# A fused cross-attention, attention and expert block: two rounds of open rows in line, the first layer norm's scaling on GpSimd

## What is computed

```
x = x + xattn(layernorm(x), ctx)     # channel gate
x = x + attn(layernorm(x))           # 32 heads of 64, 8 kv heads, causal, 64 tokens
x = x + ffn(layernorm(x))            # dense 2048 x 2048 + top-2 of 8 low-rank experts
```

```
_, topk_idx = jax.lax.top_k(cm, k)                  # cm: (16, 2048, 1601), k = 38
mask = zeros(B, L, C).at[b_idx, l_idx, topk_idx].set(1.0)
crucial = mask * x ; rest = (1 - mask) * x
# max and mean of both over the 64 channels -> conv of 7 taps -> norm -> sigmoid -> gate
```

## Time and profile before

| | us |
|---|---|
| median of 3 runs | 2354.77 (2352.66 to 2357.07) |
| the profiled execution, time | 2347.9 |
| the profiled execution, span | 2346.1 |
| PE busy / DVE busy / ACT busy / POOL busy in the span | 1996.5 / 1431.2 / 1008.6 / 930.0 |

### The profile page before, as it was taken

How to read it: one execution, slowest core, us unless ns; L and a number is a source line. 1 busy time by engine, 2 the same in 40 slices (tenths; PEclk the granted TensorE clock), 3 DMA queues, 4 the chain that set the end, 5 groups by cost and what they waited for, 6 DMA issues and landing times. The chain is left out here.

```text
span 2346.1 us, 39096 instructions
## 1 busy us (share of the span) xinstructions
PE 1996.5 (85%) x15210; PEld 1633.0 (70%) x15210; DVE 1431.2 (61%) x2343; ACT 1008.6 (43%) x2006; POOL 930.0 (40%) x855
## 2 busy tenths in 40 slices
PE   4777788788882054899999999999999999999999
PEld 4666566667762044688787888887778888878887
DVE  6999899999998898764444550134445524731111
ACT  6777767677771036432322332222333422522221
POOL 1221111112220150466554555555555535644554
PEclk9999899899996577999999999999999999999999
DMA  9999787789980203452225444322235436434443
GB/s 366 373 363 325 271 281 264 249 313 326 321 300 15 85 1 99 157 153 80 75 82 172 138 140 125 99 82 81 77 128 162 152 103 209 138 112 130 141 143 120
DMA packets 150088, 407.69 MB, mean 174 GB/s; under 512 B 15376, under 2 KB 36112, under 8 KB 148112
## 3 DMA queue, kind: packets, MB, share of 16 engines
q1 hardware_dynamic: 149616, 403.55, 50.7%
q0 software_dynamic: 288, 1.64, 0.2%
HBM read 379.96 MB, written 25.17 MB: 173 GB/s over the span
## 5 line engine op out<-in xcount | busy, mean ns | idle before, releaser
L1158 POOL TENSOR_TENSOR t<-t,t 128x512 fp32r<-128x512 f32 (+1 forms) x488 | 651.1, 1345 | 676.7 <-ACT t L1151 676.3
L1704 PE MATMUL ps<-t,t 128*128 128x512 f32 x1856 | 739.7, 399 | 19.7 <-POOL t L1158 9.4
L1706 PE MATMUL ps<-t,t 128*128 128x512 f32 x1856 | 725.4, 391 | 0.0
L1705 PE MATMUL ps<-t,t 128*128 128x512 f32 x1856 | 724.9, 391 | 0.0
L1151 ACT ACTIVATE t<-t 128x512 fp32r<-128x512 f32 (+1 forms) x488 | 295.5, 608 | 704.5 <-PE ps L1706 384.1
L704 PE MATMUL ps<-t,t 128*128 128x128 bf16 (+1 forms) x6656 | 454.0, 224 | 165.7 <-DVE t L442 155.1
L704 PEld LDWEIGHTS ps<-t,t 128*128 128x128 bf16 x6656 | 403.3, 101 | 266.7 <-DVE t L442 216.5
L442 DVE TENSOR_SCALAR t<-t,t 128x1601 bf16<-128x1601 f32 x512 | 515.7, 1050 | 3.6 <-DVE t L615 0.4
L665 ACT ACTIVATE t<-t,t 128x1601 bf16<-128x1601 f32 x256 | 416.5, 1627 | 79.4 <-DVE t L598 77.3
L1704 PEld LDWEIGHTS ps<-t,t 128*128 128x128 f32 x1856 | 349.3, 188 | 100.5 <-POOL t L1158 14.0
L1706 PEld LDWEIGHTS ps<-t,t 128*128 128x128 f32 x1856 | 349.2, 188 | 74.1
(11 more groups left out here) (214 smaller groups left out, 1698.9 us busy)
## 6 DMA issues: line engine op xcount, KB each, us to landing
t<-ctxT SPq DMA_DIRECT2D x256, 800.5 KB, 5.9
t<-wqkv SPq DMA_DIRECT2D x192, 256.0 KB, 3.2
t<-wo SPq DMA_DIRECT2D x128, 256.0 KB, 4.6
t<-wb SPq DMA_DIRECT2D x128, 256.0 KB, 3.3
t<-xT SPq DMA_DIRECT2D x32, 256.0 KB, 6.6
t<-xT SPq DMA_DIRECT2D x2, 4096.0 KB, 12.1
t<-x1d SPq DMA_DIRECT2D x32, 256.0 KB, 4.9
x2d<-t SPq DMA_DIRECT2D x32, 256.0 KB, 2.0
```

Source lines behind the costliest of these rows:

```text
L1158: e.tensor_tensor(wlo[r][:, 0:nk, :], raw[r][:, 0:nk, :], wh[r][:, 0:nk, :].bitcast(F32), ALU.subtract).then_inc(w_lo, 1)
L1704: e.matmul(bank[:, :], wh[r][:, q, :], xl, start=(kt == 0), stop=False)
L1705: e.matmul(bank[:, :], wlo[r][:, q, :], xh, start=False, stop=False)
L1706: m = e.matmul(bank[:, :], wh[r][:, q, :], xh, start=False, stop=(c == NCH[p] - 1 and q == nk - 1))
```

## The change

Two rounds of the open rows stand in line ahead of the loop, with buffers of their own (ring buffers 5, 6 and 7). The first row is picked in iteration 64, from batches 0 to 14 alone, and gathered while the last masks are made; the second is picked after the last batch's marks are there, and gathered while VectorE works on the first. The loop stays for a third round and more. `pick` now finds the largest marked position number and clears the marks from it upwards, in three instructions. The multiplications by 1 / deviation leave VectorE's iterations: GpSimd does six of them behind the first gather and ten behind the loop. The sums over channels that need them (128 matmuls) leave the search and stand ahead of `stats_tensor`. At the start, the wait of the second tile's load on GpSimd's first reduction is gone. The positions' numbers `rif` are loaded at tile 200 instead of behind the last tile.

```diff
-            if n == 1:
-                e.wait_ge(warm, 2)
...
-                if h:
-                    e.wait_ge(ln0_out, 8)
-                e.reciprocal(Rs[:, :], Mn[:, :]).then_inc(ln0_rstd, 1)
-            if LN0_MUL[h] <= i < LN0_MUL[h] + 4:
-                j = 2 * (i - LN0_MUL[h]) + late
-                e.wait_ge(ln0_rstd, h + 1)
-                e.wait_ge(ln0_sq, 16 * h + 16)
-                e.tensor_tensor(x[:, 2 * j:2 * j + 2, :], x[:, 2 * j:2 * j + 2, :], bc(Rs[:, :], 2),
-                                ALU.mult).then_inc(ln0_out, 1)
+                e.reciprocal(ln0_rs[h][:, :], Mn[:, :]).then_inc(ln0_rstd, 1)
...
+            if i == NQ:
+                first_pick_vector(e)
...
+    def ln0_out_tensor(e):
+        for h in range(2):
+            e.wait_ge(ln0_out, 8 * (h + 1))
+            for c in range(C):
+                m = xn_sums_tensor(e, C * h + c)
+            m.then_inc(xn_sum, 1)
...
+    def pick(e, do, k, upto):
+        do(e.tensor_reduce(sm[:, 8 + k:9 + k], flf[:, 0:upto], AX.X, ALU.max))
+        do(e.tensor_scalar(idx[:, k:k + 1], sm[:, 8 + k:9 + k], -1.0, 0.0, ALU.add, ALU.max))
+        do(e.scalar_tensor_tensor(flf[:, 0:upto], rif[:, 0:upto], sm[:, 8 + k:9 + k], flf[:, 0:upto], ALU.is_lt, ALU.mult))
...
+    def rows_vector(e):
+        do = in_turn(e, turn_last)
+        e.wait_ge(d_first[0], 16)
+        do(e.tensor_copy(c64[:, :], G[0][:, 0:C]))
+        largest(e, do, G[0], 0, 2)
+        e.wait_ge(counts_out, NSLOTS)
+        fin_vector(e, B - 1, range(NF))
+        e.wait_ge(fin, NF * B)
+        flags_vector(e, 1, B - 1, B)
+        e.wait_ge(flag_step, 2 * NFL)
+        do(e.tensor_tensor(flf[:, PREV:], flf[:, PREV:], rif[:, PREV:], ALU.mult))
+        pick(e, do, 1, B * NT)
+        e.sem_inc(picked, 1)
+        pick(e, do, 2, B * NT)
+        do(e.tensor_scalar(fl2[:, 0:1], sm[:, 10:11], 0.0, None, ALU.is_gt))
         e.sem_inc(flags_max, 1)
+        largest(e, do, G[0], 2, 5)
+        row_mask(e, do, 0)
+        e.wait_ge(d_first[1], 16)
+        do(e.tensor_copy(c64[:, :], G[1][:, 0:C]))
+        largest(e, do, G[1], 0, 5)
+        row_mask(e, do, 1)
...
     def rows_gpsimd(e):
+        e.wait_ge(turn_pick, 3)
+        gather_gpsimd(e, 0, d_first[0])
+        for j in range(6):
+            ln0_out_gpsimd(e, j)
+        e.wait_ge(picked, 1)
+        gather_gpsimd(e, 1, d_first[1])
+
...
-        e.memset(pend_[:, :], 0.0).then_inc(opened_p, 1)
+        for j in range(6, 16):
+            ln0_out_gpsimd(e, j)
...
         for b in range(B):
+            if b % HB == 0:
+                e.wait_ge(ln0_out, b + 8)
...
     def stats_tensor(e):
+        ln0_out_tensor(e)
         e.wait_ge(crucial, HB)
```

More of the change, by code:

```diff
@@ L245, in build @@
     M8w = M8[:, :, :, :].rearrange("p b t c -> p (b t) c").bitcast(U32)
[L247 to L259, removed]
+    G = [ring[5], ring[6], ring[7]]
+    G_TILE = [B * NT - NR + 1 + k for k in range(3)]
+    oh = at(64 * KB + 4 * RS, [256], U32)
+    c64 = at(64 * KB + 4 * RS + KB, [64])
+    eq64 = at(64 * KB + 4 * RS + KB + 256, [64])
+    prb = at(64 * KB + 4 * RS + KB + 512, [64])
+    tk = at(64 * KB + 4 * RS + KB + 768, [40])
+    w256 = at(64 * KB + 4 * RS + 2 * KB, [40])
+    mrow = at(64 * KB + 4 * RS + 2 * KB + 256, [C], U8)
     mroww = mrow[:, :].bitcast(U32)
-    rid = at(64 * KB + 4 * RS, [B, NT])
+    rif = lsq[:, B * NT:2 * B * NT]
     crc_off = 96 * KB
@@ L430, in search_sync @@
                 e.dma_start(XN[:, h, xt_, :], xT[:, h, xt_, :]).then_inc(d_x[h], 16)
[L431 to L434, removed]
+            if n == RID_TILE:
+                e.wait_ge(ln0_sqsum, 2 * NT)
+                e.dma_start(rif, rn).then_inc(d_rid, 16)
     def mask_vector(e, i, kind, u, bound):
@@ L577, in search_vector @@
     def search_vector(e):
-        for i in range(NQ + 4):
+        for i in range(NQ + 2):
             bf = (i - 6) // 4 if i >= 6 and (i - 6) % 4 in (0, 1) else None
@@ L706, in count_tensor, with ln0_out_gpsimd @@
         m.then_inc(counted, 1)
+    def ln0_out_tensor(e):
[4 more added lines that the diff above has]
+            m.then_inc(xn_sum, 1)
+    def ln0_out_gpsimd(e, j):
+        h, t = j // 8, 2 * (j % 8)
+        x = XN[:, h, t:t + 2, :]
+        e.wait_ge(ln0_rstd, h + 1)
+        e.wait_ge(ln0_sq, 16 * h + 16)
+        e.tensor_tensor(x, x, bc(ln0_rs[h][:, :], 2), ALU.mult).then_inc(ln0_out, 1)
     def search_tensor(e):
@@ L721, in build @@
                                                            sem("row_in"), sem("turn_rows"))
-    d_row = sem("d_row")
-    opened, opened_p = sem("opened"), sem("opened_p")
+    turn_pick, turn_last, picked = sem("turn_pick"), sem("turn_last"), sem("picked")
+    d_row, d_first = sem("d_row"), [sem("d_first0"), sem("d_first1")]
+    opened = sem("opened")
     rows = ctxT.rearrange("b l c -> (b l) c")
[L725 to L733, removed]
-        e.sem_inc(flags_max, 1)
@@ new lines, in first_pick_vector, with largest @@
+    def first_pick_vector(e):
+        e.wait_ge(fin, NF * (B - 1))
+        e.wait_ge(bound4, 2 * NQ)
+        flags_vector(e, 0, 0, B - 1)
+        e.wait_ge(flag_step, NFL)
+        e.wait_ge(d_rid, 16)
+        do = in_turn(e, turn_pick)
+        do(e.tensor_tensor(flf[:, 0:PREV], flf[:, 0:PREV], rif[:, 0:PREV], ALU.mult))
+        pick(e, do, 0, PREV)
+    def largest(e, do, g, r0, r1):
+        for r in range(r0, r1):
+            do(e.max(tk[:, 8 * r:8 * r + 8], g[:, :]))
+            if r < 4:
+                do(e.match_replace(g[:, :], tk[:, 8 * r:8 * r + 8], g[:, :], -FMAX))
@@ L784, in rows_gpsimd @@
         with e.While(head):
-            e.indirect_dma_start(G[:, :], None, rows, bass.IndirectOffsetOnAxis(ap=idx[:, 0:1], axis=0))\
-                .then_inc(d_row, 16)
+            gather_gpsimd(e, 2, d_row)
             e.wait_ge(d_row, 16)
```

81 lines of the change are left out of this document (34 added, 47 removed).

## The result

The changed kernel takes 2321.26 us, median of 4 runs (2319.56 to 2331.43), the kernel before on the same chip 2353.72 (2352.66 to 2357.07): ratio 0.988 (0.986 to 0.989). Run again on another chip it took 2324.21 (2320.79 to 2328.86) beside 2352.05, ratio 0.989 (0.987 to 0.990). The forecast was 2339, range 2318 to 2350; the narrower range given for the forecast without its rivals was 2330 to 2345.

What follows compares the result with a forecast made beforehand. VectorE's path up to the gate was taken as the bound, each microsecond moving the end by one. Terms -2.3 - 19.5 - 18.7 + 11.4 + 13.6 = -15.5 us on 2354.8 gave 2339, range 2318 to 2350.

Steps and rivals of the forecast that it cites:

- start: Second tile's load no longer waits for GpSimd's first reduction, so all moves up: -2.3 us.
- search to iteration 64: Multiplications and channel sums leave the search, iterations 26 to 61: -19.5 us (15.5 to 21).
- rows in line, no contention: Last mask to statistics, two open rows in line instead of loop rounds, gathers hidden: -18.7 us.
- GpSimd beside VectorE: GpSimd's multiplications hold VectorE: +11.4 us beside the last masks, +13.6 at the first row's mask and next row's copy.
- The price of a meeting: Each held VectorE instruction pays the GpSimd instruction's length less 0.22, 2.13 us for one of 2.35; masks pay in full.
- The number of meetings: Six multiplications among ten masks; behind the loop six full holds and 0.8 at the first row's mask and next copy.
- the sign that I had named for this case: If the first row's mask steps have their old lengths, the price of the lock is wrong.
- The lock costs little: Rival: masks and short steps may not be held, or GpSimd may starve; -40.5 us, 2314; chance 0.15.
- All sixteen are paid: Rival: MAX8 and MATCH_REPLACE8 wait as well, 34 - 1.4, so -7.9 us, 2347; chance 0.12.
- The gather starves: Rival: first gather's descriptors wait for all ten masks, VectorE waits 5.75 to 8 us; 2333 to 2336; chance 0.08.
- The third round: Rival "Slower": the loop runs once more and holds ten multiplications until after it; +27 us, 2382; chance 0.05 with another wait.
- The anchor: Change put on the runs' median, 6.9 us above the profiled 2347.9: 2354.8 - 15.5 = 2339, instead of 2332.

Runs made afterwards that it cites:

- repetition: The changed kernel run once more, unaltered, on another chip beside the kernel before: 2324.21 us, ratio 0.9889.
- the multiplications alone: The kernel before with only L697's multiplications and the sums over channels moved as in the change; start and open rows as before: 2384.24 us, ratio 1.0138.
- the rows alone: The changed kernel with all sixteen multiplications and the sums over channels back in the search, none on GpSimd: 2332.41 us, ratio 0.9918 to the kernel before.
- the kernel with all sixteen behind the loop: The changed kernel with all sixteen GpSimd multiplications behind the loop, none beside the last masks: 2328.38 us, ratio 0.9898 to the kernel before.
- the kernel with tiny multiplications: The changed kernel with each GpSimd multiplication cut from 2 x 512 to 2 x 8 elements a partition: 2311.99 us, ratio 0.9832 to the kernel before.
- both versions that put all of them there: The changed kernel with GpSimd's multiplications moved beside MAX8 and MATCH_REPLACE8, six or three left on VectorE: 2317.29 and 2313.92 us, ratios 0.9858 and 0.9831.

## Why the prediction was right, and which step was not

The sign, the price of a meeting and the range 2318 to 2350 held; the time was 18 us too high, outside of the forecast's own 2330 to 2345 and toward the rival to which I gave 0.15. Term by term, in us (changed kernel, and its repetition):

| term | forecast | measured | repetition |
|---|---|---|---|
| start | -2.3 | -2.0 | -2.0 |
| search to iteration 64 | -19.5 | -18.1 | -18.5 |
| rows in line, no contention | -18.7 | -17.3 | -17.3 |
| GpSimd beside VectorE | +25.0 | +13.7 | +11.4 |
| sum, at the statistics | -15.5 | -23.7 | -26.4 |

**The start and the search** were right in their sum, -20.1 and -20.5 for -21.8. 48.20 to 41.40 and to 39.40 is 6.8 and 8.8, against 6.8 and 8.7. The sums over channels gave 1.7 here and 3.2 in the repetition (201.8 to 198.6), against 3. How the sum divides is less sure than the table has it: it takes the start as it is at the first decision. Two pairs of kernels with the same start differ in the search alone, before and the multiplications alone (707.15 to 687.5) and the rows alone and the changed kernel (706.74 to 687.00): 19.7 both times, for a forecast of 19.5, which would leave 0.4 to 0.8 for the start. (The start was also rounded low: 4.35 - 1.99 is 2.36.)

**The rows in line** fell short by 1.4. The steps are as costed but for 2.9 instead of 2.6 for product and picks, 1.3 instead of 1.0 for the exit, and waits among the last masks that in the kernel with the rows alone are 0.28 and 1.51 where the earlier trace rows has 1.37; 0.4 is left.

**The price of a meeting** was right: 2.1 us, the length less 0.2, for a mask too, for which no row of before spoke. (Three GpSimd instructions in 4.76 us are one per 1.59 and not per 1.67, the first of them having been held less; 1.67 is the distance of VectorE's held steps, four in 5.71 with the first at 0.68.) **The number of meetings** was the step that failed, "five and the next row's copy let one in each": +13.6 for the first row's mask and the copy behind it, of which the run shows the copy alone; L777, L750 and L751 of the second row paid 4.9 in its place. In the last masks three and the copy L761 were held, 6.3 + 2.1, and the wait for counts was 0.3 longer: 8.7 where I had six less that wait, 11.4, since the six start 7.9 us later than I had them. The cause is the sentence "ten start about 1.5 us behind the last pick". They start 16 us behind it (730.54 to 746.71), since GpSimd pauses 7.2 us ahead of the reduction and 8.0 behind it, and so misses the first row's mask. That the steps are held as I said when they meet multiplications is shown by the kernel with all sixteen behind the loop, where these run from 729.84, 1 us ahead of that mask. The sentence behind it has a slip of its own: "nine MAX8 and MATCH_REPLACE8" do not take 9.4 us; behind the last pick there are five (747.27 to 756.71 in the earlier trace rows), and the 9.4 us are theirs. The sum does not change by it. By the sign that I had named for this case, first row's steps at their old lengths, the price of the lock would be wrong; it was right, and the place was wrong. That the multiplications missed that mask was luck and no part of the argument.

**I could have seen the pause.** At the start GpSimd's first reduction made the second tile wait 4.2 us, and ahead of the first subtraction, behind the last reduction, GpSimd was idle for 8.82, though there VectorE ended last and hid it. The Trainium skill (GPSIMD Engine Reference, Instruction dispatch) says that the first call to newly loaded code costs about 6 us with no visible instruction; the runs show 5.9 to 8.3, and at each change between reduction and multiplication, not at the first alone.

**The rivals.** "The lock costs little" is out as a price, each meeting cost 2.1; its time without any contention, -40.5, stands against some -37.7 of the kernel with tiny multiplications. "All sixteen are paid" is out: MAX8 and MATCH_REPLACE8 stay at 1.83 and 1.81 beside a multiplication, here and in both versions that put all of them there. By the rule quoted from the Trainium skill (SBUF — State Buffer, Who interferes with whom) one-input instructions outside the two-port mode are free, and masks are not; the runs agree with both (MAX8 1.83 as before, four masks 10.21 instead of 3.94). "The gather starves" is out: the row was there when VectorE came to it at 713.33, with no wait ahead of L761, and from issue to landing the first gather, beside masks, took 5.8 us and the second 5.4, where the earlier trace rows has 5.75 from issue to use. The third round didn't run; its sum, TensorE three times 28 us behind the loop, is what the multiplications alone show.

**The anchor.** I set 6.9 us on the profiled sum for the median of the runs. The terms explain only 8.2 us of the 18 (10.9 in the repetition). The medians lie 32.5 us apart and the ratio says 28.7 (26.1 in the repetition), where the conv's first step moved by 23.8 (26.5). The 6.9 us are right for before, but the changed kernel's profiled run is 10.2 above its median and the repetition's 3.4 below, so they did not carry over. A single profiled run is uncertain by that much, as the 5.9 us in the projections of the changed kernel's own trace show; where the rest of the 18 lies is open.

## What to carry to other kernels

Before you move work to GpSimd beside VectorE, list VectorE's instructions there by kind. In this kernel it was free beside MAX8, MATCH_REPLACE8 and reductions (L863 at 1.22 beside GpSimd's subtraction and alone); beside masks, copies, scans, two-input steps and predicated copies each meeting cost the length of the GpSimd instruction less 0.2 us, whatever VectorE's own. Cut the work into the free stretches and gate it on VectorE's steps; here that took the tail to 77.4 us, where it is 77.0 with no contention and 88.4 to 90.7 in the changed kernel, at the price of three multiplications left on VectorE. Count the changes between GpSimd's reduction and its elementwise work, 6 to 8 us each, and put one tiny instruction of the new kind where GpSimd is idle to take the pause early. And ask of two edits made together whether one is the cover of the other.

## What the hardware showed that I had not expected

GpSimd pauses at a change of kind: 7.1 to 8.3 us from a state that served the reduction to the first multiplication, 5.9 to 7.9 from multiplication to the next reduction; none between copy and gather, gather and reduction (0.47), or multiplication and gather and back. A multiplication of one element a partition takes the pause as well as a long one. Two MODIFY_POOL_CONFIG records stand near the start of each pause. They are not the pause themselves: in the kernel with the multiplications alone they also stand ahead of the loop's second reduction, which starts 0.1 us behind them (765.49 to 765.62), since no multiplication lies between it and the reduction before.

A hold works both ways: a multiplication beside the COPY_PREDICATED of 4.7 us lasted 6.81 us in the kernel with all sixteen behind the loop, and a reduction 4.20 instead of 0.37.

A step of VectorE on 4 elements (0.16 us alone) lasted 2.31 when it met a multiplication. Instructions of 1 element and of 40 (0.15 and 0.25) weren't held in the one place where they stood beside one.
